# x blocks of chunks 2 and 3 formed during the Q products, rotation over 1024 columns, another order ahead of the output projection

## What is computed

```python
q, k, v = apply_rope(q_in @ Wq), apply_rope(ctx @ Wk), ctx @ Wv
logits = MAX * tanh(q·k * ATTN_MULT / MAX); logits = where(mask, logits, -1e30)
x = x + (softmax(logits) @ v) @ Wo            # q_in = layernorm(x)
xf = layernorm(x)
w = softmax over the top 2 of xf @ W_router.T
x = x + xf @ W_base.T + b_base + 2 * sum_e w_e * (xf @ A_e.T) @ B_e.T
```

## Time and profile before

| | us |
|---|---|
| median of three runs | 2239.47 |
| the profiled execution, its own time | 2243.1 |
| its span, first to last instruction | 2241.3 |
| TensorE busy | 2151.8 (96%) |
| VectorE busy | 1643.2 (73%) |
| ScalarE busy | 875.9 (39%) |
| GpSimd busy | 737.4 (33%) |
| mean granted TensorE clock | 0.985 |

### The profile page before, as it was taken

The page is one execution under the profiler, slowest core; times in us unless marked ns, Lnnn a source line. Parts: engine busy times, 40 slices in busy tenths (PEclk is TensorE's granted clock), DMA queues, the critical chain, the costliest instruction groups (busy, mean ns, idle before and its releaser), DMA issues.

```text
span 2241.3 us, 26770 instructions
## 1 busy us (share of the span) xinstructions
PE 2151.8 (96%) x9429; PEld 1735.2 (77%) x9429; DVE 1643.2 (73%) x2260; ACT 875.9 (39%) x1351; POOL 737.4 (33%) x723
## 2 busy tenths in 40 slices
PE   9989877999999999988899999999999999999999
PEld 7778766888877888866677777777777777788787
DVE  5756766888887666664688788998899889854542
ACT  3223233222233111125555556655665556423221
POOL 0280632221224000002533355455545554624300
PEclk9999998999999999999999999999999999999999
DMA  8679567666668666667655575577657775586861
GB/s 288 235 219 320 199 239 277 220 218 217 218 221 300 205 207 209 225 211 244 211 186 185 186 276 191 188 242 264 238 189 234 248 254 168 171 332 236 304 228 72
DMA packets 199428, 508.52 MB, mean 227 GB/s; under 512 B 20736, under 2 KB 45952, under 8 KB 197248
## 3 DMA queue, kind: packets, MB, share of 16 engines
q1 hardware_dynamic: 175616, 432.82, 56.1%
q0 software_dynamic: 23680, 73.99, 10.2%
HBM read 357.26 MB, written 149.16 MB: 226 GB/s over the span
## 4 chain that ended last, share of the span: by engine, by line
PE 59%; issue 18%; DVE 9%; DMA 9%; ACT 2%; POOL 2%; SPq 1%; ACTq 0%; DVEq 0%; POOLq 0%
PE ps L230 19%; PE ps L232 19%; PE ps L231 19%; DMA kD<-kst 2%; DVE kRl L512 2%; DVE ql L1290 1%; PE ps L1196 1%; DMA raw<-gran 1%; POOL Xq L738 1%; DMA XcD<-T 1%; DVE Rl L1141 1%; DMA Xq<-XcD 1%; DMA kraw<-ctxT 1%; DVE kst L498 1%; DMA vE<-stg 1%
## 5 line engine op out<-in xcount | busy, mean ns | idle before, releaser
L230 PE MATMUL ps<-Ah,Rh 128*128 128x512 f32 x1024 | 401.6, 392 | 13.5 <-DVE stg L1358 4.7
L231 PE MATMUL ps<-Al,Rh 128*128 128x512 f32 x1024 | 399.7, 390 | 0.0
L232 PE MATMUL ps<-Ah,Rl 128*128 128x512 f32 x1024 | 399.6, 390 | 0.0
L1141 DVE TENSOR_TENSOR Rl<-raw,Rh 128x1024 fp32r<-128x1024 f32 x176 | 283.9, 1615 | 114.8 <-ACT Rh L1136 113.9
L230 PE MATMUL ps<-Xq,qW 128*128 128x512 f32 x896 | 351.8, 393 | 16.6 <-issue 9.3
L231 PE MATMUL ps<-Xq,qW 128*128 128x512 f32 x896 | 351.3, 392 | 0.0
L232 PE MATMUL ps<-Xq,qW 128*128 128x512 f32 x896 | 351.2, 392 | 0.0
L1136 ACT ACTIVATE Rh<-raw 128x1024 fp32r<-128x1024 f32 x176 | 185.0, 1053 | 172.0 <-PE ps L232 122.9
L230 PEld LDWEIGHTS ps<-Ah,Rh 128*128 128x128 f32 x1024 | 192.9, 188 | 60.3 <-issue 15.2
L1445 POOL DMA_DIRECT2D r<-rT x32 | 23.0, 718 | 622.1 <-ACT rT L1319 622.1
L232 PEld LDWEIGHTS ps<-Ah,Rl 128*128 128x128 f32 x1024 | 192.9, 188 | 40.9
(11 more groups left out here) (222 smaller groups left out, 4177.7 us busy)
## 6 DMA issues: line engine op xcount, KB each, us to landing
raw<-gran SPq DMA_DIRECT2D x177, 512.0 KB, 4.5
QSD<-qW SPq DMA_DIRECT2D x64, 512.0 KB, 2.9
qD<-qt SPq DMA_DIRECT2D x128, 256.0 KB, 5.7
qW<-QSD SPq DMA_DIRECT2D x64, 512.0 KB, 4.2
qf<-qD SPq DMA_DIRECT2D x64, 512.0 KB, 6.2
RB<-rD POOLq DMA_DIRECT2D x128, 256.0 KB, 4.9
qraw<-gran SPq DMA_DIRECT2D x48, 512.0 KB, 5.5
kD<-kst SPq DMA_DIRECT2D x32, 512.0 KB, 5.6
```

The source lines that it names most:

```text
L230: e.matmul(dst, lh, rh, start=first, stop=False, skip_group_check=more)
L231: e.matmul(dst, lh, rl, start=False, stop=False, skip_group_check=more)
L232: return e.matmul(dst, ll, rh, start=False, stop=last, skip_group_check=more)
L1141: t.e.tensor_tensor(l, raw[raw_of(x)][:, :], f(h), ALU.subtract).then_inc(*t.tick("w_lo", x))
```

## The change

- The x blocks of chunks 2 and 3 are no longer formed in the K and V stage (`SUMS`, `YLOAD` and `pool_kv` lose their second pair). GpSimd does it during Q in new code, `x_block`: for each of four block indices it loads four pieces (`Bx`), adds and multiplies, forms the sums and stores seven blocks. `Sq`, the place of the weight sums, becomes single; its other half is where `Bx` lies.
- x blocks 0, 1 and 2 of chunks 0 and 1 are loaded and split earlier (`sp_q_early`, `X_SPLIT`); blocks 5 and 6 are split a step later, after `q_low`.
- Each pair's banks are side by side (`qbank`), and the rotation is six operations of 1024 columns, one per step as a rule.
- Pairs 14 and 15 are interleaved otherwise; of the low parts of x of chunks 2 and 3, GpSimd makes 21 and VectorE 7 (`X_POOL`).
- Ahead of O: V's quarters come before the scores of their step, all scores and value products at other steps, other banks; V evictions first in a step, four V tiles staged in `Ah` and `Al`; the residual's loads at steps 2 to 6 and its additions at 11 to 18 in place of -1 and 2 to 9.
- In O the fourth value product of a group is one job earlier. In F the LoRA products begin at m = 7.

```diff
-        SUMS = {25: (0, 0), 26: (0, 1), 28: (0, 2), 30: (0, 3), 48: (1, 0), 49: (1, 1), 50: (1, 2), 51: (1, 3)}
+        SUMS = {25: (0, 0), 26: (0, 1), 28: (0, 2), 30: (0, 3)}
-        YLOAD = {2: 0, 32: 1}
+        YLOAD = {2: 0}
-        QP += [(n, i) for i in range(7) for n in (14, 15)]
+        QP += [(14, 0), (14, 1), (14, 2), (15, 0), (14, 3), (15, 1), (14, 4), (15, 2), (14, 5), (15, 3), (14, 6), (15, 4), (15, 5), (15, 6)]
-        qbank = [[0, 1, 2, 3], [4, 5, 6, 7]]
+        qbank = [[0, 2, 1, 3], [4, 6, 5, 7]]
...
-            for cp in range(2):
+            for cp in range(1):
...
+        XB, XB_STEP = 4, 23
...
+        def x_block(t, u):
+            e = t.e
+            k, r = divmod(u - XB, XB_STEP)
...
+            if r == 0:
+                for b in range(4):
...
+                    e.dma_start(Bx[b][:, :], xT[2 + b // 2][:, k + 4 * (b % 2), :]).then_inc(*t.tick(f"d_bx{b}", k, 16))
+            if 3 <= r < 7:
+                b = r - 3
+                y, (m, s) = Bx[b][:, :], (xl0, xl1)[b // 2]
+                t.wait_ge(f"d_bx{b}", k)
+                t.wait_ge("kv_x", (3, 1))
+                e.tensor_tensor(y, y, m[:, :], ALU.add).then_inc(*t.tick("q_xa", (k, b)))
+                t.wait_ge("q_xa", (k, b))
+                e.tensor_tensor(y, y, s[:, :], ALU.mult).then_inc(*t.tick("q_xm", (k, b)))
+            if r == 7:
+                for b in (0, 1, 3):
+                    x_store(t, k, b, 0, "q_xm", (k, b))
+            if r == 9:
...
+                e.tensor_tensor(Cc, Cc, A, ALU.subtract).then_inc(*t.tick("q_xt", (k, 0)))
+                x_store(t, k, 2, 0, "q_xt", (k, 0))
...
+        X_SPLIT = {42: 0, 44: 1, 48: 2, NK - 5: 3, NK - 3: 4}
...
+        X_POOL = [(0, 1, 2, 3)] * 4 + [(0, 1, 2), (0, 1), ()]
...
+            d = 6 if n == 31 else 2 if n in (13, 14) else 1
+            for x in range(0, 6, d):
+                TURN.setdefault(q_number[n, 6] + 1 + x // d, []).append((n, tuple(range(x, x + d))))
...
-        first = {0: ((-15, -14, -13, -12), -11, -9, (-6, -4, -3, -2)),
-                 1: ((-11, -9, -7, -6), -4, -2, (2, 3, 5, 6)),
+        first = {0: ((-14, -13, -12, -11), -10, -8, (-6, -5, -4, -3)),
+                 1: ((-10, -8, -7, -4), -2, 0, (2, 3, 5, 6)),
...
-            scores, sums, rows, values = first.get(gi, (range(z, z + 8, 2), z + 8, z + 11, range(z + 13, z + 21, 2)))
+            scores, sums, rows, values = first.get(gi, (range(z, z + 8, 2), z + 8, z + 11, (z + 13, z + 15, z + 17, z + 18)))
...
-        sbank, obank, tbank, ring = [0, 5], [2, 6], 7, [3, 1, 4]
+        sbank, obank, tbank, ring = [4, 5], [2, 6], 7, [3, 1, 0]
...
+            return (Ah, Al)[n // 2][:, 4 + 2 * (n % 2):6 + 2 * (n % 2), :] if n < 4 else stg[n % 2]
...
-                while m >= 6 and opened:
+                while m >= 7 and opened:
```

352 lines of the change are left out of this document (196 added, 156 removed).

## The result

The changed kernel takes **2183.28 us** in the median of 4 runs (2182.03 to 2188.56), the kernel before 2238.79 (4 runs, 2237.83 to 2247.77): ratio 0.9748, 95% interval 0.9718 to 0.9778. The forecast was 2175 us, with a range of 2156 to 2204, and a chance of 0.93 for faster. The profiled execution of the changed kernel is the slowest of its four, 2188.56; against the 2243.1 of the profiled one before it is 54.5 us less, where the sum of the forecast said 66.

What follows compares the result with a forecast made beforehand. TensorE, busy 2151.8 of 2241.3 us, was taken as the bound, with only idle time and slow clock to win. Terms 24 + 11 - 3 + 5 + 23 + 6 = 66 us gave 2175 us, range 2156 to 2204.

Steps and rivals of the forecast that it cites:

- K and V products: K and V products of chunks 2 and 3: TensorE's four holes there go, 24 us gained, bounds 15 and 25.5.
- V to Q: From V to Q: holes of 7.38 and 3.64 us with restarts shrink through earlier loads and splits, 11 us gained, bounds 5 and 12.
- GpSimd during Q: In Q, GpSimd's new adds, products and stores beside VectorE cost 3 us, between nothing and several us in each of four bursts.
- Rival A: GpSimd holds VectorE for two operations (11 us lost, not 3), less gained ahead of O: about 2196 us, chance 0.17.
- the sign that the prediction named for A: In the profile after, VectorE operations of over 3 us in Q with holes beside them would make A or C of it.
- the rule of one operation: The Trainium skill's rule for VectorE beside GpSimd in SBUF, exclusion by one instruction: GpSimd's term in Q would be 0, not 3.
- Rotation: Twelve operations of 512 columns become six of 1024 at 1.2 us: 0.5 to 1 us less per pair, worth nothing directly.
- Pairs 14 and 15: Second half of Q, 640 to 700 us: of 8.5 us idle and slow-clock loss, 5 gained, bounds 0 and 8.
- Ahead of O: 996 to 1100 us: of 32 us lost in holes and slow clock 9 stay, 23 gained, bounds 12 and 29.
- the prediction's own sign: In the profile after, O starts about 60 us after the last Q job, against 84 in the kernel before.
- the 8.60: TensorE's hole of 8.60 us before V's first products, waiting for pair 31's rotation; it goes when they use pair 30's banks.
- O and F: Waits of 4.1 us for the attention output's low part and 3.4 for the weighted LoRA input mostly go: 6 us gained.

Runs made afterwards that it cites:

- the run without the second pass: The kernel before without preparing the x blocks of chunks 2 and 3 in K and V, nothing moved into Q: 2210.01 us, ratio 0.9870.

## Why the prediction was right, and where it was not

The forecast holds in its main part, the holes of K and V and ahead of O. Part of the closeness is luck: losses and gains that it didn't have offset each other.

- **K and V products: right.** 24, and 7 for the start of Q, were forecast; 31.2 came, and the run without the second pass gives 34.0 by itself. Only the split was off: that term and "V to Q" have one cause. The second half of "V to Q", the hole of 3.64 at 383, did not close. The prediction priced the wait for block 5 at 1.2 us; block 5 came in time, and the stores of weight sums queued behind blocks 5 and 6 took its place (3.96 us). Of the 4 us that the table counts for it in Q, 1.5 came (jobs 0 to 6).
- **GpSimd during Q: the step that failed.** "3 us lost" was 9.2. The forecast looked at pauses between adds and products, and took the stores as bytes on a queue; it counted them, but not what their issue does to VectorE. Rival A, which held VectorE for two operations at a time and lost 11 us, had this size right, for that term alone, and the sign that the prediction named for A (VectorE operations of over 3 us in Q with holes beside them) is there. Its place was another: not every burst, but three operations that arrive during an issue, and the cost is 1.4, 2.2 and 5.4 us, not four times the same. By the rule of one operation the term would be 0, and with the stores off GpSimd that is what is measured, to 1 or 2 us.
- **Rotation: right,** 1.21 to 1.22 us per operation as taken, and worth nothing.
- **Pairs 14 and 15: too large a term.** 5 were forecast; jobs 98 to 118, where the 4.9 us of idle time and the slow clock stood, take 64.34 us in place of 66.03, and 63.91 without GpSimd's arithmetic: 2 us. A hole of 1.93 us stood at 689.96 before; one of 2.27 stands at 676.95 now. Another 1.2 us came in jobs 84 to 97, without GpSimd's arithmetic only. The order of the pairs was not tried alone.
- **Ahead of O: near in size, wrong in cause.** 17.0 us came in this stretch; that is all of the 17 if the hole at 1093.5 is counted with O, and 17 of 24 by the prediction's own sign. The banks were to bring the 8.60 and a restart; alone they bring 0.6, since half of that hole is the scores' wait for the same rotation. The residual's loads and the order of evictions were counted on too; undone, neither changes the time beyond the intervals. The places of the V tiles, named last, bring 6 to 8. The remaining 10 lie between banks with places (77.4) and the change (66.9): the later scores, value products and weights, whose parts were not separated; two holes, of 3.5 us for the rotation and 4.5 before O, go with them.
- **O and F: too small a term, and a loss that was not forecast.** Against the kernel before, the fourth value product gives 5.2 us in O and the LoRA products 3.7 in F, 8.9 where 6 were forecast. The hole at 1093.5 gave 5.6 of the 6. New waits in O for `Y` and for a weight take 3.8 back, so 10.7 came. They are also why O with the two moves undone takes 916.6 us, as long as before (915.5), though that hole isn't in it.

So the error of 11.5 us in the profile's sum is Q's 10.5 almost entirely: 6 for GpSimd's work, 2.5 for the hole behind Q's start, 3 for pairs 14 and 15, less 1 gained elsewhere. Ahead of O the sum nearly held although its reasons did not, and in O and F a loss hid a gain: that was luck, and shows that a total that agrees proves no term.

## What to carry to other kernels

When work goes to GpSimd beside a busy VectorE, ask where its DMAs are issued: give the stores to a queue that does no arithmetic. A hole that a bank causes is worth its length only if the next resource in the chain is free; look for the next product that needs the same bank, and for the second wait on the engine that evicts (here 13.2 us for stores), before pricing the first. Price a late operand in a dense stage by an experiment rather than by the sum of its recorded waits. And cut a stage into equal pieces of work in both profiles before crediting a term: whole stages add gains and losses that have nothing to do with each other.

## What was not expected of the hardware

- VectorE operations on two SBUF tiles that began about 0.2 us into GpSimd's issue of a DMA with two operations behind it were held for both in three of four cases (3.46 to 3.49 us in place of 0.68); the fourth, at 519.78, was not held. With one operation and a pause behind the issue it was 2.22 us (517.63, 575.67). The same six, shifted by some us, take 3.45 to 3.49, 0.68 and 2.22 to 2.24 us in five more profiles with the same Q stage. With the stores issued by SyncE, 1.81 us was the most.
- 28 DMA issues of 0.55 us moved from GpSimd to SyncE gained 8 us; 17 us more of VectorE work in the same stage cost nothing that the stage's length shows.
- Undoing one move brought ten recorded waits of 6.6 us and 8.1 us of stage time in O, the other one wait of 2.7 and 4.3 us in F.
